# Expert passes rewritten: routing weights spread by DMA, GpSimd scales, VectorE forms the low part

## The reference

```python
def layer0_experts(x):                 # x: tokens x 128, after a LayerNorm
    scores = sigmoid(x @ gate_w.T)
    comb = zeros(T, 16); comb[t, chosen] = scores[t, chosen]     # 4 of 16, within 2 of 4 groups
    h = silu(x @ w1.T) * (x @ w3.T)    # per expert, width 64
    return einsum('tei,edi,te->td', h, w2, comb) + shared_expert(x)

def layer1_experts(x):
    top_w, top_i = top_k(softmax(x @ router_w.T), 2); comb = top_w / sum(top_w)
    h = silu(x @ w_gate.T) * (x @ w_up.T)   # per expert, width 256
    return einsum('tei,edi,te->td', h, w_down, comb)
```

## Time and profile before

| | us |
|---|---|
| median of 3 runs | 2032.54 (2031.74 to 2033.6) |
| the profiled execution | 2030.13 |
| its span, first to last instruction | 2028.2 |
| PE busy | 1744.3 (86%) |
| DVE busy | 1439.9 (71%) |
| POOL busy | 729.4 (36%) |

### The profile page before, as it was taken

How to read it: one execution, slowest core, us unless ns; L and a number is a source line. 1 busy time by engine, 2 the same in 40 slices (tenths; PEclk the granted TensorE clock), 3 DMA queues, 4 the chain that set the end, 5 groups by cost and what they waited for, 6 DMA issues and landing times. The chain is left out here.

```text
span 2028.2 us, 28208 instructions
## 1 busy us (share of the span) xinstructions
PE 1744.3 (86%) x8712; PEld 1247.0 (61%) x8712; DVE 1439.9 (71%) x4268; ACT 960.2 (47%) x1557; POOL 729.4 (36%) x659
## 2 busy tenths in 40 slices
PE   3898959899899899977998799999967775999998
PEld 2666735555555555535766577777856564777776
DVE  5878748777777777827788567777667765677675
ACT  2444414565565555654444355555532221555554
POOL 3444421312312312124445455555521001555555
PEclk9999968999999999987999899999978887999999
DMA  3000011111111111010000100000000000000000
GB/s 103 1 1 0 1 29 22 26 22 27 21 22 30 18 22 28 12 39 37 0 1 0 40 1 1 1 0 0 1 0 0 0 1 1 1 11 6 5 11 11
DMA packets 18248, 28.08 MB, mean 14 GB/s; under 512 B 2753, under 2 KB 10178, under 8 KB 18130
## 3 DMA queue, kind: packets, MB, share of 16 engines
q1 hardware_dynamic: 15874, 23.68, 5.4%
q10 hardware_dynamic: 2256, 2.96, 0.5%
HBM read 10.83 MB, written 2.10 MB: 6 GB/s over the span
## 5 line engine op out<-in xcount | busy, mean ns | idle before, releaser
L976 ACT ACTIVATE att_probs<-banks 128x1024 f32<-128x1024 f32 (+3 forms) x384 | 305.9, 811 | 197.1 <-PE banks L887 195.3
L1101 DVE CUSTOM_DVE_ANT_0 banks<-banks,att_mask 128x128 f32<-128x128 f32 (+3 forms) x512 | 234.3, 525 | 73.5 <-PE banks L868 73.0
L868 PE MATMUL banks<-arena 128*128 128x512 f32 (+3 forms) x768 | 250.1, 407 | 27.5 <-DMA arena<-att_parts 15.1
L1016 POOL TENSOR_SCALAR_AFFINE_SELECT att_probs<-att_probs 128x512 f32<-128x512 f32 x128 | 81.2, 635 | 422.7 <-ACT att_probs L976 422.7
L868 PEld LDWEIGHTS banks<-arena 128*128 128x128 f32 x768 | 133.1, 198 | 151.6 <-issue 91.9
L461 POOL TENSOR_TENSOR ffn1b_hid_l<-ffn1b_hid,ffn1b_hid_h 128x512 fp32r<-128x512 f32 x128 | 165.0, 1292 | 130.0 <-ACT ffn1b_hid_h L415 130.0
L461 POOL TENSOR_TENSOR ffn1a_hid_l<-ffn1a_hid,ffn1a_hid_h 128x512 fp32r<-128x512 f32 x128 | 165.3, 1293 | 125.2 <-ACT ffn1a_hid_h L415 125.2
L887 PE MATMUL banks<-arena 128*128 128x512 f32 (+3 forms) x768 | 205.2, 352 | 0.5 <-ACT att_probs L976 0.4
L1103 DVE TENSOR_REDUCE att_mx<-banks 128x1 f32<-128x512 f32 x256 | 162.2, 684 | 32.0 <-PE banks L868 31.8
L906 PE MATMUL banks<-att_probs,att_v_aug 128*32 128x512 f32 (+3 forms) x1536 | 167.7, 509 | 0.6 <-POOL att_probs L1016 0.5
L887 PEld LDWEIGHTS banks<-arena 128*128 128x128 f32 x768 | 137.7, 191 | 26.4 <-ACT att_probs L976 11.3
(11 more groups left out here) (404 smaller groups left out, 4176.3 us busy)
## 6 DMA issues: line engine op xcount, KB each, us to landing
arena<-att_parts SPq DMA_DIRECT2D x16, 384.0 KB
arena<-att_parts SPq DMA_DIRECT2D x128, 48.0 KB
w_raw<-in_ffn_w_dram SPq DMA_DIRECT2D x6, 352.0 KB, 5.5
out_dram<-x SPq DMA_DIRECT2D x8, 256.0 KB, 2.3
setup_raw<-in_ffn_w_dram SPq DMA_DIRECT2D x3, 576.0 KB, 6.4
w_raw<-in_ffn_w_dram SPq DMA_DIRECT2D x3, 320.0 KB, 6.2
setup_raw_sel<-in_consts_dram ACTq DMA_DIRECT2D x1, 576.0 KB, 10.9
x<-in_L_attn_x_dram ACTq DMA_DIRECT2D x1, 512.0 KB, 8.0
```

The costliest lines, as they stand in the source:

```text
L868: mm = pe.matmul(bank[:, at:at + width], q_st[:, n % 3, t * P:(t + 1) * P], k_pad[:, n % 2, j, c * G:c * G + width], start=True, stop=True ...
L976: act.activation(probs[:, unit % NPROB, 2 * pair:2 * pair + 2, 0:c], score_ps[:, pair, :, 0:c], ACT.Exp, scale=SCALE).then_inc(exped, 1)
L1101: ins = dve.tensor_tensor_reduce(now, now, mask[:, G - width:G], 1.0, -3e38, ALU.add, ALU.max, best)
```

## The change

`phase_moe` is written anew. The matmul with `sel`, its PSUM bank, the `sel` matrices and their loads are gone, and so are the two DVE instructions that split the weights into high and low parts. In their place SP issues DMAs inside SBUF: when `combt` of a group is there, it copies each expert's row of 512 weights onto all the partitions of that expert's rows in a new tile `share` (8 slots of 128 x 512 fp32). In layer 0 a slot takes two DMAs, each from one row of `combt` to 64 partitions; in layer 1 one DMA from one row to 128 partitions. POOL now multiplies `sil` by `share` (`scale`), in place of DVE; the shared expert's chunk has no scaling. DVE now forms the low part of `hid` (`low`), in place of POOL, behind the `hide` of the chunk after it. PSUM and SBUF buffers of gate, up, `sil`, `scl`, `hid` become three instead of two (`NB`, `NH`). The LayerNorm's last step moves from DVE to ACT, with a small product on POOL ahead of it, and statistics are made two groups ahead. The loop over groups is unrolled. `SplitAhead` keeps three staged pieces of 512 columns in place of all at once, and the pieces are issued by SP between the groups.

```diff
+    SLOTS = 8
     PER = 1 if first else I1 // P
...
+    NSCALED = SLOTS * PER
+    HALVES = P // I0 if first else 1
+    LAG = 2
+    NB, NH = 3, 3
...
-        cstack, combt = sb("cstack", [P, TG, P]), sb("combt", [P, 2, G], F32R)
...
-        gate_ps, up_ps, comb_ps = k.banks[:, 0:2, :], k.banks[:, 2:4, :], k.banks[:, 4:6, :]
...
+        combt, share = sb("combt", [NE, 2, G]), sb("share", [P, SLOTS, G])
...
+        gate_ps, up_ps, y_ps, misc = k.banks[:, 0:3, :], k.banks[:, 3:6, :], k.banks[:, 6, :], k.banks[:, 7, :]
...
+            for g in range(g0, end):
+                sp.wait_ge(comb_t, g + 1)
+                for e in range(SLOTS):
+                    if g > g0:
+                        sp.wait_ge(scaled, (g - 1) * NSCALED + (e + 1) * PER)
+                    for h in range(HALVES):
+                        n, at = e * HALVES + h, h * P // HALVES
+                        sp.dma_start(share[at:at + P // HALVES, e, :],
+                                     combt[n:n + 1, g % 2, :].unsqueeze(1).broadcast_to([1, P // HALVES, G]))\
+                          .then_inc(share_in[e], 16)
+                if out is not None and g > g0:
+                    store(g - 1)
+                for c in range(NC):
+                    if piece_at(g + 1, c) is not None:
+                        ahead.load(sp, piece_at(g + 1, c))
...
-                if c % PER == 0:
-                    e = c // PER
-                    if c == 0:
-                        pe.wait_ge(comb_t, g + 1)
-                    mm = pe.matmul(comb_ps[:, comb_bank(q, c), :], sel[:, e * P:(e + 1) * P], combt[:, q, :],
-                                   start=True, stop=True)
...
+            def norm(g):
+                act.wait_ge(rstd_done, 2 * g + 2)
+                for t in range(TG):
+                    ins = act.activation(xn[:, t, :], k.x[:, tile_of(g, t)], ACT.Identity, bias=nshift[:, t:t + 1],
+                                         scale=rstd[:, t:t + 1])
+                ins.then_inc(norm_done, 1)
...
-                pool.tensor_tensor(hid_l[:, n, :], hid[:, n, :], hid_h[:, n, :].bitcast(F32), ALU.subtract)\
-                    .then_inc(low_cut, 1)
...
+                pool.wait_ge(silu_done, num + 1)
+                at_least(pool, hidden, num - NB + 1)
+                if c % PER == 0:
+                    pool.wait_ge(share_in[c // PER], (g + 1) * HALVES * 16)
+                pool.tensor_tensor(scl[:, num % NB, :], sil[:, num % NB, :], share[:, c // PER, :], ALU.mult)\
+                    .then_inc(scaled, 1)
...
-                dve.tensor_copy(cstack[:, :, 0:NE].bitcast(F32R), comb[:, :, 0:NE]).then_inc(comb_high, 1)
-                dve.wait_ge(comb_high, g + 1)
-                dve.tensor_tensor(cstack[:, :, 32:32 + NE].bitcast(F32R), comb[:, :, 0:NE],
-                                  cstack[:, :, 0:NE], ALU.subtract).then_inc(route, 1)
...
-                dve.tensor_tensor(scl[:, n, :], sil[:, n, :], comb_ps[:, comb_bank(q, c), :], ALU.mult).then_inc(scaled, 1)
...
+                if c < NSCALED:
+                    dve.wait_ge(scaled, g * NSCALED + c + 1)
+                else:
+                    dve.wait_ge(silu_done, num + 1)
                 dve.wait_ge(up_done, num + 1)
...
+            def low(num):
+                dve.wait_ge(high_cut, num + 1)
+                dve.tensor_tensor(hid_l[:, num % NH, :], hid[:, num % NH, :], hid_h[:, num % NH, :].bitcast(F32),
+                                  ALU.subtract).then_inc(low_cut, 1)
...
+                        hide(h, c)
+                        if h * NC + c > g0 * NC:
+                            low(h * NC + c - 1)
```

More of the change, by code:

```diff
@@ L251, in phase_moe @@
-        block = ctx.enter_context(nc.Block())
[L253 to L269, removed]
-                        sp.dma_start(out.rearrange("b (n p) d -> p (b n) d", p=P)[:, g * TG:(g + 1) * TG, :],
-                                     k.x[:, g * G:(g + 1) * G].rearrange("p (n d) -> p n d", d=D)).then_inc(stored, 16)
-                    sp.wait_ge(stored, 16 * NG)
+        block = ctx.enter_context(nc.Block())
@@ L334, in yturn @@
-            def yturn(g, more):
+                if c == 0:
+                    at_least(pe, y_out, g)
+                pe.wait_ge(low_cut, num + 1)
+                pe.matmul(y_ps, down_h[:, ws], hid_h[:, num % NH, :], start=c == 0, stop=False)
+                pe.matmul(y_ps, down_l[:, ws], hid_h[:, num % NH, :], start=False, stop=False)
+                pe.matmul(y_ps, down_h[:, ws], hid_l[:, num % NH, :], start=False, stop=c == NC - 1)\
+                    .then_inc(down_done, 1)
+            def yturn(g):
@@ L335, in yturn @@
                 pe.wait_ge(y_out, g + 1)
-                if more:
+                if g + 2 < end:
                     if first:
@@ L344, in yturn @@
                 mm.then_inc(y_turned, 1)
[L346 to L347 removed]
+            for h in range(g0 - 2, end):
                 for c in range(NC):
[L349 to L360 removed]
@@ L464, in body @@
-            def body(g, q, more):
-                start = isinstance(g, int) and g == g0
-                for c in range(NC):
-                    if c > 0:
-                        low(g, q, c - 1)
-                    elif not start:
-                        low(g - 1, 1 - q, NC - 1)
-                    if place(g, c) is not None:
-                        ahead.low(pool, place(g, c))
-                    if more and slot["rstd"] == c:
-                        invert(g + 1)
+                pool.wait_ge(silu_done, num + 1)
@@ L484, in _ @@
-            body(g0 + NG - 2, 0, True)
-            body(g0 + NG - 1, 1, False)
-            low(g0 + NG - 1, 1, NC - 1)
+            for h in range(g0 - 2, end):
+                for c in range(NC):
+                    if h >= g0:
+                        if c < NSCALED:
+                            scale(h, c)
+                        if piece_at(h, c) is not None:
+                            ahead.low(pool, piece_at(h, c))
+                    chain(h, c, (("rstd", invert),))
         @block.vector
@@ L616, in body @@
[L616 to L628 removed]
+                dve.tensor_tensor(hid[:, num % NH, :], (scl if c < NSCALED else sil)[:, num % NB, :],
+                                  up_ps[:, num % NB, :], ALU.mult).then_inc(hidden, 1)
@@ L648, in parcel @@
+            low(end * NC - 1)
+            add(end - 1)
 def parcel(arena):
```

449 lines of the change are left out of this document (189 added, 260 removed).

## The result

The changed kernel takes 3289.81 us (median of 4, 3284.37 to 3292.26) against 2032.76: ratio 1.6181, 95% interval 1.6153 to 1.6209. The forecast was slower, 3480, with 3280 to 3730; the time lies at the range's low end, 190 us under the forecast. The profiled execution took 3291.62 us, with a span of 3289.9.

What follows compares the result with a forecast made beforehand. Single-partition DMA transfers at 27.0 GB/s were taken to bound the passes: ffn0a +409, ffn0b +408, ffn1a +315, ffn1b +316, setup -2, so +1446 on 2030.1 gives 3476; median 2.4 higher, so 3480 us, range 3280 to 3730.

Steps and rivals of the forecast that it cites:

- What bounds, and the rate: Expert passes: DMA transfers into `share`, each from one partition at 27.0 GB/s, set the length of every group.
- 77.7 us for a group: Filling `share`: 2.097 MB a group at 27.0 GB/s, in both layers; eight groups end to end make 621.6 us a pass.
- rates between: Rival: the DMA engines drift apart over slots and use several groups of four at once; 2300 to 3280 us, chance 0.05.
- The sign that I named: Next profile: layer-0 and layer-1 groups differing much in length would mean that the bytes do not set it.
- Nor does the queue run dry: Turn between groups: PE reaches it with 4 to 5 us of the last slot's transfer still to go, so no gap.
- Ends of a pass, other traffic, setup: Around the transfers: ends about 8 us a pass; other queue traffic 8, 1 and 5 us; setup -2 us.
- Issue at 0.673 us: SP's issue of each DMA inside SBUF: 10.8 us a group in layer 0, 5.4 in layer 1, less than a group takes.
- where I had written 1680: Next profile: PE busy about 1680 us, half the span, its granted clock down at 0.5 in much of the passes.
- my two prices: Rivals with transfers hidden: about 2000 us if the loop decides, 2090 if DVE and POOL block each other; chance 0.05 each.
- The loop and its 2.6 us a chunk: Gate, Silu, POOL's scale, hide, low and back to PE: 5.17 us for two chunks, 2.6 for one.
- my price has 197 / 8 = 24.6: Layer-0 pass with transfers hidden: 8 x (8 x 2.6 + 2) plus some 14 of routing, 197 us.
- my 2.74 us a chunk: Rival where DVE and POOL block each other: scale, hide and low run one after another; 2090 us, chance 0.05.

Runs made afterwards that it cites:

- one limit in layer 1: Changed kernel with layer 1's eight source rows on partitions 0 to 3 and 32 to 35 instead of 0 to 7: 3348.5 us.
- turned earlier: Changed kernel with the next group's weights turned one chunk earlier (chunk 6 for 7 in layer 0, 12 for 13 in layer 1): 3201.4 us.
- The hidden case: Changed kernel with each expert's row repeated in `combt`, so that a DMA reads 8 or 16 partitions: 2234.6 us.
- LAG 3: Changed kernel with DMAs reading 8 or 16 partitions, plus the down product three places behind gate and up instead of two: 2049.7 us.
- groups of their own: Changed kernel with each expert's source row on a separate group of four neighbouring partitions, still one partition per DMA: 2444.9 us.
- four neighbours: Changed kernel with each expert's row four times on neighbouring partitions, all read by one DMA: 2577.5 us.
- twenty apart: Changed kernel with each expert's row four times, on partitions n, n+20, n+40, n+60, all read by one DMA: 2192.1 us.
- the swap: Changed kernel with DMAs reading 8 or 16 partitions, plus scaling back on DVE and low back on POOL: 2048.6 us; with LAG 3 too, 1987.4 us.

## Why the prediction was right, and where its sizes were off

*What bounds, and the rate.* Right. The queue, not an engine, sets each group; 27 GB/s inside a slot is what was taken from the earlier trace rows, and where nothing overlaps (one limit in layer 1) a group takes 77.0 and 79.6 us against the 77.7 forecast. That eight partitions, not four, share it changed nothing here, as the source rows 0 to 15 lie in four such sets.

*"77.7 us for a group", no two DMAs side by side.* Mis-sized. The rival "rates between" said that engines could drift apart over slots in different groups of four, and I gave it 0.05 since each DMA is cut evenly; they do so at every border inside a group, for 2.5 us. My range went down to 3280 "with some overlap between slots", without a size for it. The groups came to 69.9, 69.6, 74.9 and 74.9 us, which over eight each is 172 us less than 77.7: nearly all of the 184 between the sum (3476) and the profiled 3291.6. The sign that I named, unequal layer-0 and layer-1 groups, was there, and meant this.

*"Nor does the queue run dry."* Wrong step. I let PE reach the turn 4 to 5 us before the last transfer ends. It reaches it at about that end: the copy of turned weights starts at 174.4 us, the engines' share is 0.12 from 174 to 175 us and 0.00 from 175 to 176. Worth 88 us (turned earlier), hidden in the total by the larger error of the other sign. That the time lies in the range is in part luck: 3289.8 is 10 us above its lower end, and the same kernel without the holes takes 3201.4, below it.

*Ends of a pass, other traffic, setup.* The passes were 568.9, 566.4, 609.2 and 610.8 us against 631, 639, 632 and 636; with the groups' 172 taken off, 11 are left for all ends and loads together. Right within that.

*Issue at 0.673 us.* Not what SP shows now: the median L270 in ffn0a spans 4.8 us. It costs nothing, since SP waits there for the queue's own pace.

*PE.* The clock did fall (0.68 to 0.82 over the passes, 0.50 in many windows), but PE's busy time rose to 2073.7 where I had written 1680: a matmul at the lower clock is busy longer (0.63 us each in the rows at 1508 us, 0.40 in the earlier trace rows). POOL waited for the DMA 448.7 us in the eight groups of ffn0a, 56 each, where over 60 was named.

*Rivals.* The hidden case is neither of my two prices: it takes 2234.6, not 2000 or 2090. The loop and its 2.6 us a chunk were right (2.58 in a group without routing work, 185 us gone with LAG 3). Left out was the routing work, which stands inside a loop without slack: 9.5 and 10.2 us in a layer-1 group, some 138 us over the 14 that have it. Layer 0 was too cheap as well, with groups of 29.1 and 30.2 us where my price has 197 / 8 = 24.6, some 80 us; that part was not taken apart. DVE and POOL do block each other, but my 2.74 us a chunk is not shown: I had put scale, hide and low one after another, and hide runs beside the scale. A limit of each single partition is refuted by the run with groups of their own, and by four neighbours against twenty apart.

## What to carry to other kernels

A DMA inside SBUF that repeats one partition ran at about 27 GB/s here, with 128 KB and with 256 KB alike: copy the source onto many partitions first (partition + 32 adds nothing). PE's turn gives that almost for nothing; the copy of the turned weights takes 0.597 us in place of 0.587. Before a move is called hidden, work out the loop that it leaves behind, and what other work stands in it. When an edit that should help is buried under a larger bound, test it on top of a version without that bound: LAG 3 and the swap are worth 61 us with the bound and 247 without it.

## What was not expected of the hardware

A DMA whose source is four partitions used about four of the sixteen DMA engines (share 0.20 to 0.23), against 0.79 with one source partition in the same place. Partitions 32 apart share a limit: four sources made of two such pairs moved 52 GB/s over 140 us, four without such a pair 74.
